# Preparing the later layers' weights beside the expert-choice routing in a five-stage audio tower

## The chip, the cores and the metric

The kernel runs on one core of one Trainium2 chip. The metric is the device time of one execution in microseconds; the time given is the median of three runs. All arithmetic is float32. Where a matmul needs full precision, an operand is rounded to a shorter format ("hi", type fp32r) and the remainder is kept beside it ("lo"); three matmuls then stand for one.

## The reference

The input x is (16, 750, 128). Five steps follow one another on h of (16, 748, 128), each but the first as h = h + f(layernorm(h)):

```python
h = tok(x, kernel)                       # convolution of width 3, then c = f*c + (1-f)*z, h = o*c
h = h + cross_attention(ln(h))           # 8 heads of 16, batch b attends to batch (b + 8) % 16
h = h + expert_choice(ln(h))             # 8 experts of 256; each takes its best 187 tokens of 748
h = h + slice_attention(ln(h))           # 8 heads of 64, 32 slices
h = h + mixture(ln(h))                   # 2 shared experts of 512, and the best 2 of 8 routed ones
```

Slice attention uses W_in, b_in, Wq, Wk, Wv, W_out and b_out. Because softmax is the only non-linear step, products of these weights are formed once (`wqk`, `fold`, and three biases). The mixture has `sw1, sw2` (shared), `rw1, rw2` (routed) and a gate. Layernorm has no learned parameters: it needs a mean and a reciprocal deviation for every token.

## The kernel before

`audio_tower` (line 2552 on) runs the stages strictly one after the other: `quasi_recurrent`, `cross_attention`, `expert_choice`, `slice_attention`, `mixture`. Each stage is made of blocks. In a block the five engines and SyncE's DMA queue have programs of their own, tied by semaphores; a block ends when all of them are done, and after a group of blocks another one clears its semaphores. So nothing of a later block overlaps an earlier one. h stays in SBUF as 96 tiles of 128 tokens (16 batches of 6 tiles); `g.stats` holds six numbers for every tile.

**Weights and statistics.** `weights_and_statistics` (line 102 on) loads weight pieces into a ring of four (line 142), turns them on TensorE where needed (line 154), rounds them to hi on ScalarE (line 170) and subtracts for lo on VectorE (line 186). A load waits until the piece four before it has its lo. With `taken` False, VectorE runs the 96 `bn_stats` (line 189) between its pieces. Lines 193 to 203 then make mean and deviation: seven small VectorE operations and a square root on ScalarE. Expert choice calls it with `taken` False, the other stages with True, because the work that made their h also took its statistics.

**Cross attention** works in 32 units (a batch and half of the heads), each of six steps. TensorE interleaves `probe` matmuls for the next unit's row maxima (line 750), score matmuls (line 770) and the sums with v (line 786). VectorE reduces every probe (line 840) out of a ring of three PSUM banks. TensorE may fill a bank only once VectorE has released the probe three places before it. After a unit's 48 probes VectorE makes `neg_max` (line 845), TensorE turns it, VectorE copies it to `max_rows` (line 850), and a DMA places it in the next unit's q stack (line 705); the next unit waits for that (`row_loaded`). GpSimd adds a unit's output to h (line 680).

**Expert choice**: weights and statistics, `router_logits`, `route`, then `gated_ffn`. `route` (line 1031 on) is one chain on VectorE: a softmax, and 24 rounds of `max` (line 1106) and `match_replace` (line 1111). ScalarE has one exponential in it, TensorE one group of transposes, GpSimd nothing, and SyncE stores the gates at its end (line 1118).

**Slice attention** begins with `slice_weights` (line 1481 on): weights and statistics, `load_small` with four loads, and a block with 8 matmuls for `wvo`, 40 for the products, and their evictions. **The mixture** begins with `expert_records` (line 1961 on): 16 weight pieces of 256 KB are turned, split into hi and lo and stored to the DRAM tensor `records` in stores of 512 KB. SyncE issues the load of piece j, then waits for the lo of piece j-2 and issues its store. Then come weights and statistics for the shared experts and the gate, one small load, a one-instruction block, `router_logits`, `dispatch` and `experts`.

Of the kernel before, what the change touches and what calls it, by code (L numbers as in the profile page):

```python
# [5 lines left out]
F32 = mybir.dt.float32  # L6
# [5 lines left out]
P = 128  # L12
# [568 lines left out]
def cross_attention(nc, g, w):  # L581

    with ExitStack() as ctx:
# [78 lines left out]
        with nc.Block() as block:  # L662
# [168 lines left out]
            def _(dve):  # L831
                def take(u, item, at, bank):
# [198 lines left out]
def route(nc, g, logits, gates, k_tokens, k_experts, tag):  # L1031
# [4 lines left out]
    with ExitStack() as ctx:  # L1036
# [21 lines left out]
        with nc.Block() as block:  # L1058
# [375 lines left out]
def expert_choice(nc, g, w):  # L1434
# [4 lines left out]
    with ExitStack() as ctx:  # L1439
# [10 lines left out]
        with ExitStack() as inner:  # L1450
# [10 lines left out]
            ], "c", False)  # L1461
            router_logits(nc, g, wg_hi, wg_lo, None, logits, "c")
            route(nc, g, logits, gates, K_TOKENS, None, "c")
# [17 lines left out]
def slice_weights(nc, g, w, wqk_hi, wqk_lo, fold, bias_q, bias_k, bias_out):  # L1481

    with ExitStack() as ctx:
        def sb(name, shape, dt=F32):
            return ctx.enter_context(nc.sbuf_tensor(name, shape, dt))

        def psum(name, shape):  # L1490
            return ctx.enter_context(nc.psum_tensor(name, shape, F32))

        sem = semaphores(nc, ctx)

        win_t = sb("win_t", [S_DIM, S_HEADS, P])
        wv_t = sb("wv_t", [S_DIM, 1, S_DIM])
        b_col = sb("b_col", [S_DIM, 1, S_HEADS])
        wqk = sb("wqk_raw", [S_DIM, 2, SLICES])
        w_out = sb("w_out_raw", [S_DIM, S_HEADS, P])
        b_out = sb("b_out_rows", [P, P])  # L1500
        b_wide = sb("b_wide", [S_DIM, S_HEADS, P])
        wvo = sb("wvo", [S_DIM, S_HEADS, P])
        weights_and_statistics(nc, g, [
            (win_t[:, :, :], None, w["L1_attn_W_in"].rearrange("d (h k) -> d h k", k=S_DIM), True),
            (wv_t[:, :, :], None, w["L1_attn_Wv"].rearrange("k (o c) -> k o c", o=1), True),
            (b_col[:, :, :], None, w["L1_attn_b_in"].rearrange("(h o k) -> h o k", o=1, k=S_DIM), True)], "d", True)
        load_small(nc, [
            (wqk[:, 0, :], w["L1_attn_Wq"], None), (wqk[:, 1, :], w["L1_attn_Wk"], None),
            (w_out[:, :, :], w["L1_attn_W_out"].rearrange("(h k) o -> k h o", k=S_DIM), None),
            (b_out[:, :], w["L1_attn_b_out"].unsqueeze(0).broadcast_to([P, P]), None)], "d")  # L1510
        p_vo = psum("p_vo", [S_DIM, 2, 4, P])
        p_qk = psum("p_qk", [P, S_HEADS, 2, SLICES])
        p_fold = psum("p_fold", [P, 2, 4, P])
        p_bq = psum("p_bq", [P, S_HEADS, SLICES])
        p_bo = psum("p_bo", [P, 2, P])
        p_bk = psum("p_bk", [P, 2])
        widened, vo_done, vo_kept, rest_done, rounded = (
            sem(s) for s in ("b_widened", "vo_done", "vo_kept", "rest_done", "wqk_rounded"))
        with nc.Block() as block:
            @block.tensor  # L1520
            def _(pe):
                for h in range(S_HEADS):
                    last = pe.matmul(p_vo[:, h // 4, h % 4, :], wv_t[:, 0, :], w_out[:, h, :], start=True, stop=True)
                last.then_inc(vo_done, 1)
                pe.wait_ge(widened, 1)
                pe.wait_ge(vo_kept, 1)
                for h in range(S_HEADS):
                    at = slice((h % 4) * SLICES, (h % 4 + 1) * SLICES)
                    pe.matmul(p_qk[:, h, :, :], win_t[:, h, :], wqk[:, :, :], start=True, stop=True)
                    pe.matmul(p_fold[:, h // 4, h % 4, :], win_t[:, h, :], wvo[:, h, :], start=True, stop=True)  # L1530
                    pe.matmul(p_bq[:, h, :], b_wide[:, h, :], wqk[:, 0, :], start=True, stop=True)
                    pe.matmul(p_bo[at, h // 4, :], b_wide[:, h, 0:SLICES], wvo[:, h, :], start=True, stop=True)
                    last = pe.matmul(p_bk[at, h // 4:h // 4 + 1], wqk[:, 1, :], b_col[:, 0, h:h + 1],
                                     start=True, stop=True)
                last.then_inc(rest_done, 1)

            @block.vector
            def _(dve):
                dve.tensor_copy(b_wide[:, :, :], b_col[:, 0, :].unsqueeze(2).broadcast_to([S_DIM, S_HEADS, P])
                                ).then_inc(widened, 1)  # L1540
                dve.wait_ge(vo_done, 1)
                dve.tensor_copy(wvo[:, :, :], p_vo[:, :, :, :].rearrange("p a b o -> p (a b) o")).then_inc(vo_kept, 1)
                dve.wait_ge(rest_done, 1)
                for j in range(2):
                    dve.scalar_tensor_tensor(out=bias_out[:, j, :], in0=b_out[:, :], scalar=1.0 / S_HEADS,
                                             in1=p_bo[:, j, :], op0=ALU.mult, op1=ALU.add)
                dve.tensor_copy(bias_k[:, :], p_bk[:, :])
                dve.tensor_copy(fold[:, :, :], p_fold[:, :, :, :].rearrange("p a b o -> p (a b) o"))
                dve.wait_ge(rounded, 3)
                for j in range(2):  # L1550
                    dve.tensor_tensor(wqk_lo[:, j, :].rearrange("p (h s) -> p h s", s=SLICES), p_qk[:, :, j, :],
                                      wqk_hi[:, j, :].bitcast(F32).rearrange("p (h s) -> p h s", s=SLICES), ALU.subtract)
                dve.tensor_tensor(bias_q[:, 1, :].rearrange("p (h s) -> p h s", s=SLICES), p_bq[:, :, :],
                                  bias_q[:, 0, :].bitcast(F32).rearrange("p (h s) -> p h s", s=SLICES), ALU.subtract)
# [1036 lines left out]
```

## Time and profile before

| | |
|---|---|
| three runs | 3235.11, 3237.22, 3238.65 us (median 3237.22) |
| the profiled execution | 3239.33 us; its span 3237.6 us |
| mean granted TensorE clock | 0.932 of full speed |
| busy, share of the span | TensorE 87%, VectorE 74%, ScalarE 58%, GpSimd 31% |

A row of the timeline begins with its start and length in us, then the engine (PE TensorE, PEld its weight loads, DVE VectorE, ACT ScalarE, POOL GpSimd, SPq SyncE's DMA queue), the line, the operation, what it writes and reads, and in brackets how long the engine was idle before it and what ended that. "x3" means that a row merges three instructions. A row of windows gives busy time and, in brackets, counts, for each engine, then the granted TensorE clock (1.00 is 2.4 GHz, 0.50 is 1.2 GHz), the DMA engines' share and GB/s.

### The profile page before, as it was taken

How to read it: one execution, taken by the hardware profiler on the slowest of the kernel's cores; microseconds unless marked ns; L12 is line 12 of the kernel's file. 1: busy time of each engine (PE TensorE's matmuls, PEld its weight loads, DVE VectorE, ACT ScalarE, POOL GpSimd, SP SyncE). 2: the span in 40 equal slices, each digit the busy share in tenths (PEclk: the TensorE clock that was granted, in tenths of full speed). 3: DMA queues.
4: the chain of work that ended last, by engine and by line, in shares of the span. 5: the costliest groups of instructions: out<-in, count | busy, mean ns of one | idle time of the engine just before them, and what ended most of it. 6: DMA issues, size and time to landing. Idle time of an engine off the chain costs nothing. (4 is left out here: it accounts for less than half of the span.)

```text
span 3237.6 us, 56270 instructions
## 1 busy us (share of the span) xinstructions
PE 2806.1 (87%) x16922; PEld 2239.5 (69%) x16922; DVE 2397.2 (74%) x4399; ACT 1872.4 (58%) x3098; POOL 1005.0 (31%) x873
## 2 busy tenths in 40 slices
PE   8975999999999999419999999588855899799994
PEld 8975665665666665319999999488844688688883
DVE  4544888888888886778999999377738666578775
ACT  3343466666666666308888888144422677577773
POOL 0033000000000000204555555233302577466664
PEclk9988899999999999759999999699967899899997
DMA  1138444355344341002322222220040211277767
GB/s 51 33 141 275 60 67 61 49 64 62 51 60 65 52 56 23 27 15 77 91 84 86 85 86 90 88 99 0 0 169 2 89 48 48 91 239 245 241 192 228
DMA packets 149262, 290.48 MB, mean 90 GB/s; under 512 B 23006, under 2 KB 77981, under 8 KB 142220
## 3 DMA queue, kind: packets, MB, share of 16 engines
q1 hardware_dynamic: 135564, 264.13, 33.4%
q0 software_dynamic: 13568, 24.75, 2.3%
q8 instruction: 65, 1.06, 0.1%
q14 instruction: 65, 0.53, 0.1%
HBM read 203.15 MB, written 87.11 MB: 90 GB/s over the span
## 5 line engine op out<-in xcount | busy, mean ns | idle before, releaser
L840 DVE TENSOR_REDUCE part_max<-to_dve 128x1 f32<-128x374 f32 (+1 forms) x1536 | 744.0, 540 | 163.3 <-PE to_dve L750 148.6
L902 ACT ACTIVATE probs<-score 128x748 f32<-128x748 f32 x768 | 579.7, 794 | 403.9 <-PE score L770 402.5
L750 PE MATMUL to_dve<-k_stack,q_stack 127*128 127x374 f32 (+1 forms) x1536 | 509.7, 377 | 30.9 <-DMA k_stack<-k_parts 30.8
L750 PEld LDWEIGHTS to_dve<-k_stack,q_stack 127*128 127x128 f32 (+1 forms) x1536 | 272.7, 190 | 299.6 <-DVE part_max L840 252.4
L2460 DVE TENSOR_TENSOR m_hid_lo<-m_hid,m_hid_hi 128x512 fp32r<-128x512 f32 x408 | 289.8, 711 | 161.3 <-ACT m_hid_hi L2433 161.3
L770 PE MATMUL score<-q_stack,k_stack 128*128 128x374 f32 x1536 | 395.1, 339 | 0.0
L1357 DVE TENSOR_TENSOR f_hid_lo_c<-f_hid_c,f_hid_hi_c 128x748 fp32r<-128x748 f32 x256 | 350.0, 1376 | 42.6 <-ACT f_hid_hi_c L1340 39.6
L680 POOL TENSOR_TENSOR h<-h,o_rows 128x256 f32 (+2 forms) x96 | 49.4, 531 | 944.9 <-DVE o_rows L863 944.9
L1253 POOL TENSOR_TENSOR f_acc_c<-f_acc_c,f_gate_c 128x748 f32<-128x748 f32 x112 | 253.1, 2259 | 259.6 <-DVE f_gate_c L1373 259.3
L786 PE MATMUL o_sum<-probs,v_sb 128*17 128x374 f32 (+1 forms) x3072 | 315.9, 483 | 16.4 <-ACT o_cols L893 14.0
L1335 ACT ACTIVATE f_hid_c<-f_up_c,c_b 128x374 f32<-128x374 f32 x512 | 268.5, 571 | 76.3 <-DVE f_hid_lo_c L1357 52.0
L770 PEld LDWEIGHTS score<-q_stack,k_stack 128*128 128x128 f32 x1536 | 274.3, 191 | 9.1 <-ACT probs L902 7.8
L2356 POOL DMA_INDIRECT e_sums<-m_gated,m_row_in x216 | 213.3, 987 | 163.8 <-DVE m_gated L2478 110.4
L2433 ACT CAST m_hid_hi<-m_hid 128x512 fp32r<-128x512 f32 x408 | 248.3, 609 | 0.0
L2350 POOL DMA_INDIRECT e_slots<-e_rows,e_places x192 | 195.5, 1018 | 103.2 <-issue 57.1
L1340 ACT CAST f_hid_hi_c<-f_hid_c 128x748 fp32r<-128x748 f32 x256 | 209.5, 819 | 9.9
L2440 ACT ACTIVATE m_hid<-m_up,m_weights 128x512 f32<-128x512 f32 x216 | 148.8, 689 | 91.1 <-PE m_up L2389 91.1
L2440 ACT ACTIVATE m_hid<-m_up,e_b 128x512 f32<-128x512 f32 x192 | 132.2, 688 | 96.4 <-PE m_up L2389 96.4
L1274 PE MATMUL f_up_c<-f_hi_c,c_w_hi 128*128 128x374 f32 x512 | 181.0, 353 | 6.5 <-ACT f_hid_c L1335 5.3
L2389 PE MATMUL m_up<-m_hi,m_weights 128*128 128x512 f32 x432 | 175.0, 405 | 0.0
L2399 PE MATMUL m_down<-m_hid_hi,m_weights 128*128 128x512 f32 x432 | 170.7, 395 | 1.4 <-DVE m_hid_lo L2460 1.4
L1274 PE MATMUL f_up_c<-f_hi_c,c_w_lo 128*128 128x374 f32 x512 | 171.4, 335 | 0.0
(412 smaller groups left out, 6170.9 us busy)
## 6 DMA issues: line engine op xcount, KB each, us to landing
m_weights<-e_records SPq DMA_DIRECT2D x54, 1028.0 KB, 6.8
f_gate_c<-c_gates SPq DMA_DIRECT2D x128, 374.0 KB, 3.4
q_stack<-q_parts SPq DMA_DIRECT2D x128, 187.0 KB, 5.4
k_stack<-k_parts SPq DMA_DIRECT2D x128, 187.0 KB, 9.4
e_slots<-blank SPq DMA_DIRECT2D x54, 260.0 KB, 3.6
m_row_in<-e_slots SPq DMA_DIRECT2D x54, 260.0 KB, 3.0
m_weights<-e_sums SPq DMA_DIRECT2D x16, 640.0 KB
e_records<-rec_parts SPq DMA_DIRECT2D x16, 512.0 KB, 3.9
```

The source lines that it names most:

```text
L750: last = pe.matmul(ring[bank][0:ROWS[c], 0:HALF], q_stack[its_slot][0:MAX_ROW, head, c * P:c * P + ROWS[c]], k_stack[its_slot][0:MAX_ROW, ...
L770: last = pe.matmul(score[e % 2][:, m, 0:HALF], k_stack[slot][:, head, c * P:(c + 1) * P], q_stack[slot][:, head, HALVES[half]], start=True ...
L786: last = pe.matmul(o_sum[head * LANE:head * LANE + VCOLS, 0:HALF], v_sb[slot][0:ROWS[c], c, head, :], probs[0:ROWS[c], s % 2, head, m, :], ...
L840: dve.tensor_reduce(part_max[0:ROWS[c], head, c, half:half + 1], ring[bank][0:ROWS[c], 0:HALF], AX.X, ALU.max).then_inc(used, 1)
L902: act.activation(probs[:, s % 2, head, :, :], score[e % 2][:, :, 0:HALF], ACT.Exp).then_inc(prob_done, 1)
L1253: pool.tensor_tensor(acc[:, slot, :], acc[:, slot, :], place, ALU.add).then_inc(summed, 1)
L1274: last = pe.matmul(up[h][:, 0:HALF], a[:, k, :], m[:, slot, cols], start=(i == 0), stop=(i == 2))
L1335: act.activation(hid[:, k % 2, cols], up[h][:, 0:HALF], ACT.Gelu, bias=b1[:, 0, k:k + 1]).then_inc(gelu_done, 1)
L1357: dve.tensor_tensor(hid_lo[:, k % RING, :], hid[:, k % 2, :], hid_hi[:, k % RING, :].bitcast(F32), ALU.subtract).then_inc(lo_done, 1)
L2433: act.copy(hid_hi[:, f % RING, :], hid[:, f % RING, :]).then_inc(hi_done, 1)
L2440: act.activation(hid[:, f % RING, :], up[f % UPS][:, :], ACT.Gelu, bias=up_bias(m, f - starts[m])).then_inc(gelu_done, 1)
L2460: dve.tensor_tensor(hid_lo[:, f % RING, :], hid[:, f % RING, :], hid_hi[:, f % RING, :].bitcast(F32), ALU.subtract).then_inc(lo_done, 1)
```

## The change

Four things are changed.

1. **Statistics of cross attention.** VectorE takes three `bn_stats` at the end of step 4 (of 0 to 5) in every unit from the third on, over tiles that two units before it finished, after a wait on GpSimd's additions; the last six follow the last unit. Expert choice calls `weights_and_statistics` with `taken` True.
2. **One list of later weights.** `later_weights` prepares everything that `slice_weights`, `expert_records` and the mixture's own call did. It returns a program for each engine, and `route` runs them in its block: on TensorE after the group of transposes, on ScalarE after the exponential, on GpSimd at once, on SyncE ahead of the wait for the gates. VectorE has no part of it.
3. **Other engines for the split.** ScalarE now copies every piece out of PSUM twice (hi, and the whole), and GpSimd subtracts. 13 small loads come first, then 20 pieces of 256 KB (4 shared, 16 routed) in a ring of four, and 16 stores. The product matmuls stand between pieces 3 and 4. PSUM has a ring of four banks for all of it.
4. **The old places.** `slice_weights`, `expert_records`, both `load_small` calls and the one-instruction block are gone. `slice_attention` and `mixture` call `weights_and_statistics` with an empty list, which leaves the operations of lines 193 to 203.

```diff
@@ cross_attention, vector engine
+                def take_tiles(first, n):
+                    for j in range(n):
+                        at = bass.ds(first + j, 1)
+                        dve.bn_stats(g.stats[:, at, :]..., g.h[:, at, :]...)
                     for s, items in enumerate(plan(u)):
                         for k, item in enumerate(items):
                             take(u, item, *number(u, s, k))
+                        if s == STEPS - 2 and at_least(u, 2):
+                            dve.wait_ge(added, u * 2)
+                            take_tiles(u * SPAN - 2 * SPAN, SPAN)        # SPAN = 3
...
+                dve.wait_ge(added, 2 * UNITS)
+                take_tiles((UNITS - 2) * SPAN, 2 * SPAN)
@@ route
             def _(sp):
+                later.sync(sp)
                 sp.wait_ge(whole, 1)
                 sp.dma_start(gates, gate_cols[:, :]).then_inc(kept, 16)
+                later.end(sp)
                 sp.wait_ge(kept, 16)
...
                 act.activation(flat, flat, ACT.Exp).then_inc(exped, 1)
+                later.scalar(act)
...
                 turn_tiles(pe, g, turn, src).then_inc(turned, 1)
+                later.tensor(pe)
+            @block.gpsimd
+            def _(pool):
+                later.gpsimd(pool)
@@ later_weights (new)
+    def sync(sp):
+        def store(n):
+            if kind == "shared":
+                return
+            sp.wait_ge(lo_done, n + 1)
+            sp.dma_start(records[x, ...], parts[:, n % RING, ...]).then_inc(stored[n % RING], 16)
+        for dst, src in small:                                            # 13 of them
+            sp.dma_start(dst, src).then_inc(small_in, 16)
+        for n, (kind, x, side) in enumerate(pieces):                      # 4 shared, 16 routed
+            if n >= RING:
+                sp.wait_ge(turned, job_of(n - RING) + 1)
+            sp.dma_start(raw[:, n % RING, :, :], view).then_inc(raw_in[n % RING], 16)
+            if n >= LATE:                                                 # LATE = 2
+                store(n - LATE)
+        for n in range(len(pieces) - LATE, len(pieces)):
+            store(n)
+        sp.wait_ge(evacuated, SMALL_JOB + 1)
+        sp.dma_start(records[:, :, 4 * HID_E:REC]..., records_bias[:, :, :]).then_inc(bias_stored, 16)
+    def end(sp):
+        sp.wait_ge(bias_stored, 16)
+        for j in range(RING):
+            sp.wait_ge(stored[j], 16 * (len(pieces) - OWN) // RING)
+    def tensor(pe):
+        pe.wait_ge(small_in, 16 * len(small))
+        ...  # 7 small transposes, 8 of W_in, pieces 0 and 1, 8 matmuls for wvo, pieces 2 and 3,
+        ...  # 40 product matmuls, pieces 4 to 19 (4 transposes each)
+    def scalar(act):
+        def round_piece(n):
+            act.wait_ge(turned, j + 1)
+            act.copy(piece_at(n)[0], heads4(j))
+            act.copy(whole[:, n % RING, :, :], heads4(j)).then_inc(evacuated, 1)
+    def gpsimd(pool):
+        def low_piece(n):
+            pool.wait_ge(evacuated, job_of(n) + 1)
+            pool.tensor_tensor(lo, whole[:, n % RING, :, :], hi.bitcast(F32), ALU.subtract).then_inc(lo_done, 1)
@@ slice_attention, mixture
-        slice_weights(nc, g, w, wqk_hi, wqk_lo, fold, bias_q, bias_k, bias_out)
+        weights_and_statistics(nc, g, [], "d", True)
-        expert_records(nc, g, w, records)
...
-            weights_and_statistics(nc, g, [ ...gate, ups, downs, sb2, sb1... ], "e", True)
-            load_small(nc, [...gate_b...], "e")
+            weights_and_statistics(nc, g, [], "e", True)
```

## Rows read from the trace of the kernel before

**Rows 1.** windows of core 0: one row for each of five stretches

```profile
318.00:1307.20 989.20, 964.78 (x6368) 587.28 (x6368) 795.96 (x1792) 595.56 (x832) 49.39 (x96) 0.98 0.43 56
1309.00:1338.60 29.60, 0.56 (x2) 0.35 (x2) 26.20 (x119) 7.57 (x15) 0.00 (x0) 0.50 0.25 72
...
1389.30:1452.10 62.80, 1.51 (x6) 1.14 (x6) 54.33 (x83) 2.12 (x2) 0.00 (x0) 0.50 0.02 6
...
2054.20:2075.60 21.40, 19.95 (x96) 18.27 (x96) 1.90 (x2) 0.00 (x0) 0.00 (x0) 0.50 0.00 1
2373.00:2439.20 66.20, 22.18 (x85) 15.53 (x85) 16.88 (x35) 13.53 (x23) 0.00 (x0) 0.51 0.61 207
```

**Rows 2.** timeline inside cross attention, from one unit to the next

```profile
884.25 1.00 DVE L840 TENSOR_REDUCE part_max<-to_dve 128x1 f32<-128x374 f32 x2
...
885.17 0.27 DVE L850 CAST max_rows<-to_dve 24x128 fp32r<-24x128 f32 x1
...
885.30 0.61 PE L750 MATMUL to_dve<-k_stack,q_stack 127*128 127x374 f32 x2
885.47 0.77 SPq L705 DMA_DIRECT2D q_stack<-max_rows  x1
...
887.91 0.37 PEld L770 LDWEIGHTS score<-q_stack,k_stack 128*128 128x128 f32 x2
```

**Rows 3.** groups of instructions, VectorE, 1308 to 1339 us: busy, mean | idle

```profile
L189 DVE BATCH_NORM_STATS2 stats<-h 128x6 f32<-128x128 f32 x96 | 19.9, 276 | 0.0
```

**Rows 4.** timeline and DMA issues (KB each, us to landing), expert choice's weights

```profile
1309.50 14.50 SPq L142 DMA_DIRECT2D raw_c<-in_L_ffn_W_dram  x12
...
1338.65 0.34 POOL L952 MEMSET c_wg_hi<- 128x120 f32 x2 [31.55 <-POOLq L54]
...
raw_c<-in_L_ffn_W_dram SPq DMA_DIRECT2D x4, 256.0 KB, 2.7
```

**Rows 5.** timeline, first and last of the routing block, and the next stage

```profile
1389.72 0.95 DVE L1069 TENSOR_REDUCE peak_c<-c_logits 128x96 f32<-128x768 f32 x1 [1.52 <-PEq L54]
...
1448.67 0.37 SPq L1118 DMA_DIRECT2D c_gates<-gate_cols_c  x1
...
1452.15 1.47 POOL L90 TENSOR_TENSOR f_rows_c<-h,mean 128x768 f32<-128x768 f32 x1 [73.55 <-POOLq L54]
```

**Rows 6.** timeline, from the block after the feed-forward to slice attention

```profile
2039.36 0.06 DVE L177 MEMSET eps_d<- 128x1 f32 x1 [2.12 <-PEq L54]
...
2044.40 0.31 DVE L193 TENSOR_TENSOR diff_d<-stats 128x96 f32<-128x96 f32 x1
...
2046.33 0.75 DVE L203 RECIPROCAL rstd<-std_d 128x96 f32<-128x96 f32 x1 [0.44 <-ACT std_d L172]
...
2079.09 0.20 POOL L1647 MEMSET first_row<- 128x128 f32 x1 [45.72 <-POOLq L54]
```

**Rows 7.** timeline, from the block after slice attention to the mixture's router

```profile
2375.56 0.11 DVE L2036 MEMSET rec_bias<- 128x64 f32 x1 [2.69 <-PEq L54]
...
2379.37 2.82 PE L2023 MATMUL rec_turn<-ident,rec_raw 128*128 128x128 f32 x12 [1.64 <-DMA rec_raw<-in_L_ffn_rw_dram]
...
2418.59 0.43 SPq L2007 DMA_DIRECT2D e_records<-rec_bias  x1
...
2439.27 0.33 POOL L952 MEMSET e_wg_hi<- 128x120 f32 x2 [75.40 <-POOLq L2542]
```

**Rows 8.** waits of SyncE's DMA queue, 2374 to 2424 us: total, times, longest

```profile
SPq L1990 <- DVE rec_parts L2043: 26.9, 14, 4.2
```

**Rows 9.** single lines: duration ns min/median/max, first and last start us

```profile
L770 PE MATMUL score<-q_stack,k_stack x1536: 327/334/515, 348.1 to 1300.2; 128*128 128x374 f32 x192
...
L962 POOL TENSOR_TENSOR r_rows_c<-r_rows_c,rstd x16: 612/613/614, 1340.9 to 1378.0; 128x256 f32<-128x256 f32 x16
...
L92 POOL TENSOR_TENSOR y_rows<-y_rows,rstd x16: 1468/1471/1473, 202.3 to 271.7; 128x768 f32<-128x768 f32 x16
...
L1357 DVE TENSOR_TENSOR f_hid_lo_c<-f_hid_c,f_hid_hi_c x256: 919/1148/2562, 1463.0 to 2027.0; 128x748 fp32r<-128x748 f32 x128
```

More of the change, by code:

```diff
@@ L1028, in _, with route @@
                                           ALU.add)
-def route(nc, g, logits, gates, k_tokens, k_experts, tag):
+def route(nc, g, logits, gates, k_tokens, k_experts, tag, later):
     N = B * TILES
@@ L1431, in _, with expert_choice @@
                 sp.wait_ge(done, 16 * len(loads))
-def expert_choice(nc, g, w):
+def expert_choice(nc, g, w, records, d, e):
     HID = 256
@@ L1460, in expert_choice @@
                 (b1[:, :, :], None, w["L0_ffn_b1"].rearrange("e (j o f) -> (e j) o f", o=1, f=P), True),
-            ], "c", False)
+            ], "c", True)
             router_logits(nc, g, wg_hi, wg_lo, None, logits, "c")
-            route(nc, g, logits, gates, K_TOKENS, None, "c")
+            with ExitStack() as beside:
+                route(nc, g, logits, gates, K_TOKENS, None, "c", later_weights(nc, beside, g, w, records, d, e))
         gated_ffn(nc, g, w1_hi, w1_lo, b1, w2_hi, w2_lo, b2, None, BLOCKS, 0, gates, None, "c")
@@ L1478 @@
 HS = S_HEADS * SLICES
[L1481 to L1554, printed above, removed]
-            @block.scalar
-            def _(act):
-                act.wait_ge(rest_done, 1)
-                for j in range(2):
-                    act.copy(wqk_hi[:, j, :].rearrange("p (h s) -> p h s", s=SLICES), p_qk[:, :, j, :]
-                             ).then_inc(rounded, 1)
-                act.copy(bias_q[:, 0, :].rearrange("p (h s) -> p h s", s=SLICES), p_bq[:, :, :]).then_inc(rounded, 1)
@@ L1565, in slice_attention, with slice_storage, sb, mixture_storage @@
-def slice_attention(nc, g, w, slots):
+def slice_storage(nc, ctx):
+    d = Shared()
+    def sb(name, shape, dt=F32):
+        return ctx.enter_context(nc.sbuf_tensor(name, shape, dt))
+    d.wqk_hi, d.wqk_lo = sb("wqk_hi", [P, 2, HS], F32R), sb("wqk_lo", [P, 2, HS], F32R)
+    d.fold = sb("fold", [P, S_HEADS, P])
+    d.bias_q = sb("bias_q", [P, 2, HS], F32R)
+    d.bias_k = sb("bias_k", [P, 2])
+    d.bias_out = sb("bias_out", [P, 2, P])
+    return d
+def mixture_storage(nc, ctx):
+    e = Shared()
+    def sb(name, shape, dt=F32):
+        return ctx.enter_context(nc.sbuf_tensor(name, shape, dt))
+    n = SHARED * UNIT
+    e.w1_hi, e.w1_lo = sb("e_w1_hi", [P, n, P], F32R), sb("e_w1_lo", [P, n, P], F32R)
+    e.w2_hi, e.w2_lo = sb("e_w2_hi", [P, n, P], F32R), sb("e_w2_lo", [P, n, P], F32R)
+    e.b1 = sb("e_b1", [P, 1, n])
+    e.b2 = sb("e_sb2", [P, 1])
+    e.gate_bias = sb("e_gate_b", [P, E_N])
+    e.wg_hi, e.wg_lo = sb("e_wg_hi", [P, 1, WIDE], F32R), sb("e_wg_lo", [P, 1, WIDE], F32R)
+    return e
@@ L2504, in _, with mixture @@
                     add_pair(b)
-def mixture(nc, g, w, slots, out):
+def mixture(nc, g, e, records, slots, out):
     N = B * TILES
-    BLOCKS = SHARED * UNIT
     with ExitStack() as ctx:
@@ L2526, in mixture @@
         with ExitStack() as inner:
[L2527 to L2529 removed]
             logits = inner.enter_context(nc.sbuf_tensor("e_logits", [P, TILES, B, E_N], F32))
[L2531 to L2546 removed]
+            weights_and_statistics(nc, g, [], "e", True)
+            router_logits(nc, g, e.wg_hi, e.wg_lo, e.gate_bias, logits, "e", rows)
             dispatch(nc, g, logits, rows, places, second, table)
[L2548 to L2549 removed]
+        experts(nc, g, records, slots, sums, rows, places, second, table, e.w1_hi, e.w1_lo, e.w2_hi, e.w2_lo, e.b1,
+                e.b2[:, 0:1], out)
 def audio_tower(nc, w, out):
@@ L2561, in audio_tower @@
         cross_attention(nc, g, w)
-        expert_choice(nc, g, w)
         slots = nc.dram_tensor("e_slots", (ROUTED * BLOCK, RECORD), F32, kind="Internal").ap()
-        slice_attention(nc, g, w, slots)
-        mixture(nc, g, w, slots, out)
+        records = nc.dram_tensor("e_records", (E_N, P, REC), F32, kind="Internal").ap()
+        e = mixture_storage(nc, ctx)
+        with ExitStack() as sliced:
+            d = slice_storage(nc, sliced)
+            expert_choice(nc, g, w, records, d, e)
+            slice_attention(nc, g, d, slots)
+        mixture(nc, g, e, records, slots, out)
 _INS = ['x', 'L0_tok_kernel', 'L0_attn_q_w', 'L0_attn_kv_w', 'L0_ffn_Wg', 'L0_ffn_W1', 'L0_ffn_b1', 'L0_ffn_W2',
```

300 lines of the change are left out of this document (193 added, 107 removed).

## The prediction

> **What bounds the kernel now.** The blocks follow one another, so a stretch of time is worth what the wait that ends last in it allows. The first view is the windows by stage [rows 1]. In cross attention TensorE is busy 965 of 989 us and VectorE 796: no VectorE work added there is free by itself. Four stretches look different. Expert choice's weights (29.6 us) have VectorE busy 26.2, TensorE nearly idle. The routing block (62.8 us) is one VectorE chain, 54.3 us busy, while the other engines and the DMA do nothing. The weights ahead of slice attention (the 41.7 us after the feed-forward) and ahead of the mixture (66.2 us, DMA share 0.61) are stages that no token needs: only their statistics depend on h. The second view is the timeline at the edges of these stretches [rows 4 to 7]. It gives what each costs from start to start, block boundaries included. The third is the timeline inside cross attention [rows 2], and the fourth SyncE's waits in the record stage [rows 8], which tell what sets the pace of the pieces.
>
> **Slice attention's weights, removed.** GpSimd's first operation of slice attention stands at 2079.09, the block after the feed-forward opens at 2039.36 [rows 6]. With an empty list the block has only the statistics. These took from 2044.40 to 2047.08 [rows 6], 2.7 us, and one boundary follows. For its price I take 1.06 us, what lies between the end of expert choice's statistics, 1337.59, and 1338.65, the next stage's first operation [rows 4]. The new start is 2039.36 + 0.1 + 2.7 + 1.06 = 2043.2, so the change gives 35.9 us. After it the low clock is no new cost: the granted clock is 0.50 in the old stretch even with TensorE busy 20 of 21.4 us [rows 1], so slice attention started cold already.
>
> **The mixture's preparation, removed.** By the same sum: block open at 2375.56, router's first operation at 2439.27 [rows 7], new start 2375.56 + 3.84 = 2379.4. It gives 59.9 us. Both sums have an uncertainty of 1 to 2 us, the boundaries.
>
> **Expert choice without `bn_stats`.** 96 of them are 19.9 us of VectorE, 0.207 each [rows 3], in a stage of 29.6. Not all of it comes back, because the loads are next late. A load waits for the lo four pieces before it. SyncE's first twelve issues took 14.5 us [rows 4]. In the chain of piece 0, 4, 8 and 12 a link of 128 KB is about 3.1 us (landing, 0.4 of ScalarE, 0.4 of VectorE), and the last, of 256 KB, about 4.8 (2.7 us landing [rows 4], behind three like it). Piece 0 has its lo some 2 us after the first issue, at 1311.1. So: 1311.1 + 3.1 + 3.1 + 4.8 = 1322.1, then 0.6 for the two bias copies and 2.7 of statistics, 1325.4 instead of 1337.6. I take a gain of 12.2 us; ends 10 (every landing 0.5 later) and 19.9 (VectorE still the bound).
>
> **The same `bn_stats` in cross attention.** The last six follow the last addition to h, outside any cover: 6 x 0.207 = 1.3 us. The other 90 come three to a unit, 0.62 us, after `neg_max`. What is queued behind them on VectorE are the first two probes of step 5 and `max_rows`, and TensorE waits for these through the ring. VectorE took the two probes at 884.25, TensorE issued the next two at 885.30 [rows 2]. It may do so when each of the first two is released, at about 884.75 and 885.25, so the slack is 0.2 us at the second. With 0.62 to 0.75 more (0.75 if the address arithmetic does not run ahead) TensorE loses 0.4 to 0.55. The maxima's row is the other path: issued at 885.47, it is needed at 887.91 [rows 2]. A DMA of that size should land near 887.5; it moves by 0.62 and TensorE by 0.45, so it stays just hidden. TensorE has next to no idle time in this stage, so a stall is not won back. I take 0.5 us in each of 29 units, 14.5 us. The ends are 0 (three banks cover it) and 0.95 a unit (all of it, plus a late row), 28 us.
>
> **The new work in routing.** Here the question is whether it fits beside the chain of VectorE, which runs from 1389.72 to 1448.6 [rows 5]. SyncE begins with 13 small issues. One costs between 0.37 [rows 5] and 0.77 [rows 2]; I take 0.5, 6.6 us. TensorE waits for all 13: with 2.3 us of landing (2.7 for 256 KB [rows 4]) it starts at 1398.6. Ahead of the first routed piece stand 31 transposes at 2.82/12 = 0.235 us [rows 7], 7.3 us, and the 48 matmuls of the products, which took 20 of the 21.4 us [rows 1]. First routed piece: 1425.9. The 16 routed pieces took from 2379.37 to 2418.59 before, 39.2 us or 2.45 a piece [rows 7]. They have the same bytes now, three loads are again ahead of them, and SyncE has the same order. SyncE waited for lo there, 26.9 us in 14 times [rows 8], so the path from load to lo sets the pace, at least in part. It grows by ScalarE's second copy (0.5) and by GpSimd in place of VectorE. GpSimd takes 0.61 us for 256 elements and 1.47 for 768 [rows 9], hence 1.04 for 512, against 0.69. That is 0.85 in a loop that carries three pieces, with handing over some 1.0: up to 0.33 a piece. If the DMA alone sets the pace it is 0. I take 0.2: 3.2 us, and 1.1 once for the longer last piece. The last store is out at about 1469.5. The gates' store stands behind it on SyncE: issue at 1470. From that issue to GpSimd's next stage it was 3.5 us (1448.67 to 1452.15 [rows 5]); 1.0 more for stores still in flight and 1.0 for one more block that clears semaphores give 1475.4 instead of 1452.15. The work does not fit: it costs 23.3 us, of which the 59 us beside VectorE are the cover used. Ends: 12 (DMA pace, issues of 0.4) and 33 (0.33 a piece, 10 us of small issues, a GpSimd that also waits). VectorE itself has 20 us to spare here.
>
> GpSimd and VectorE run side by side for the first time in this block. With GpSimd's additions running in the feed-forward, VectorE's two-input subtraction goes from 919 ns to a median of 1148 and up to 2562 [rows 9]. If the rounds of `max` and `match_replace` were stretched likewise, VectorE's chain would grow by at most GpSimd's own busy time, some 25 us, to about 1474: just the end that SyncE has anyway. So it costs nothing more either way. The Trainium skill (SBUF — State Buffer, the sections on the shared port pair) says that only VectorE operations with two SBUF inputs or in a two-port mode contend with GpSimd, and that a loser blocks for a whole instruction. By it the rounds, one input each, are not stretched; without it the sum is the same. No row of this trace has a `max` beside GpSimd.
>
> **Sum.** -35.9 - 59.9 - 12.2 + 1.3 + 14.5 + 23.3 = -68.9 us. From the profiled execution's own 3239.3 us (its span 3237.6 and 1.7 around it) that is 3170.4. The median of the three runs is 2.1 us below the profiled one, hence 3168.
>
> **The rivals.**
> - *The ring covers the statistics.* Then cross attention pays only 1.3 us: 3168 - 14.5 = 3154. For it: VectorE is idle for a fifth of the stage, 796 busy of 989 us [rows 1]. Against: the slack at the place where the three stand is 0.2 us [rows 2]. Chance 0.18.
> - *They cost all and the row comes late.* 0.8 to 0.95 a unit, 3177 to 3181. For it: the row's landing isn't shown, and 2.4 us is close. Chance 0.14.
> - *Routing hides more.* If the small issues are short, the products are faster in their new grouping, and the DMA sets the pace, the excess falls to 8 to 12 us: 3153 to 3157. Hiding all of it would need the routed pieces at 1.4 us each, with 768 KB moved for each, and these rows show 2.45 [rows 7]. Chance 0.14.
> - *Routing stretches more*, to 30 us or above, because GpSimd's subtractions are slower than 1.04: 3175 to 3182. Chance 0.10.
> - *The other side: cross attention loses its clock.* The stage stands on a granted clock of 0.98 [rows 1]. If the new stalls made the grant drop for part of it, a score matmul goes from 334 to 515 ns [rows 9], and TensorE-bound time grows by at least half of the stretch so spent. To eat the gain of 69 us some 140 of the 989 us must fall to the low level, 4 to 5 us in every unit. That gives 3237 and more; less than that stays a gain. Against: the stage keeps 0.98 although TensorE waits in every unit already, and the added stall is 0.5 us in 30. Chance 0.02.
> - *The change doesn't do what it says*: the later weights end up behind the routing instead of beside it. In part this is my forecast; if all of it stood behind (86 us), the time would be about 3232. The programs start without waiting for VectorE's rounds, so I give it 0.01.
>
> **How the numbers follow.** The forecast itself, 3168 with its own spread of 6 either way, has 0.41. The cases below it reach to 3147, those above to 3186, and the range from 3147 to 3186 leaves out about 0.15. Faster by over 0.2%, about what a measurement of this kernel can tell from no change, is all but two rivals: 0.97; within it 0.01; slower 0.02.
>
> **What would show it.** Cross attention's stretch should be some 16 us longer, with TensorE's probes of step 5 late behind `max_rows`. Expert choice's weights should last about 16 to 17 us. In routing, VectorE should be done at about 59 us from its first operation and then idle for some 20 while SyncE still stores records; a next stage that starts within 5 us of VectorE's last operation would prove the excess wrong. From block opening to slice attention, and to the mixture's router, it should be some 4 us each. The forecast is wrong if a unit of cross attention grows by less than 0.2 or more than 0.9 us, or if the pieces come faster than 2.3 or slower than 3.0 us.

## The result, and the profile after

The changed kernel takes **3228.0 us** (median of 14 runs, 3222.1 to 3236.3) against 3236.1 before (14 runs, 3233.6 to 3238.7): a ratio of 0.9975, with a 95% interval of 0.9967 to 0.9982. That is 8 us faster, where 68 were forecast. Its profiled execution took 3223.5 us, with a span of 3221.4. One run of an experiment below, of after_no_stats, took 9296.7 us; it is left out of its figures as slow, and nothing here tells why.

Stage by stage, from the timelines of both kernels (us; before by [rows 1, 4 to 7], after by the rows below):

| stage | before | after | change | forecast |
|---|---|---|---|---|
| cross attention, up to expert choice's weights | to 1309.2 | to 1390.2 | +81.0 | +15.8 |
| expert choice's weights, to the router's first operation | 29.5 | 17.9 | -11.6 | -12.2 |
| routing block, to the feed-forward's first operation | 62.4 | 80.1 | +17.6 | +23.3 |
| feed-forward to slice attention's first operation | 39.7 | 3.8 | -36.0 | -35.9 |
| slice attention to the mixture's router | 63.7 | 3.8 | -59.9 | -59.9 |
| all others (mixture -6.0, feed-forward -0.9, routers and slice attention -0.4) | | | -7.3 | 0 |

The sum is -16.2, the difference of the two spans. It is more than the 8 us between the medians, because the profiled execution of before lies 3 us above its median and that of after 4.6 below. The mixture's 6.0 are in part scatter: over all profiles here it took 794.0 to 798.3 us in the five with its old code (mean 796.1) and 791.4 to 794.2 in the nine with the new (mean 793.3); what the other 3 us are was not looked for. So the changed stages came near the forecast, routing 6 us better, and the gain went into cross attention. After's timeline where these stages begin and end (start, us of the row, engine, line, operation):

```profile
1390.20 0.06 DVE L177 MEMSET eps_c<- 128x1 f32 x1 [2.02 <-PEq L54]
...
1406.25 0.75 DVE L203 RECIPROCAL rstd<-std_c 128x96 f32<-128x96 f32 x1 [0.44 <-ACT std_c L172]
...
1408.06 0.34 POOL L965 MEMSET c_wg_hi<- 128x120 f32 x2 [21.18 <-POOLq L54]
...
1458.96 0.95 DVE L1082 TENSOR_REDUCE peak_c<-c_logits 128x96 f32<-128x768 f32 x1 [1.52 <-PEq L54]
...
1539.02 1.47 POOL L90 TENSOR_TENSOR f_rows_c<-h,mean 128x768 f32<-128x768 f32 x1 [6.89 <-POOLq L54]
...
2125.34 0.06 DVE L177 MEMSET eps_d<- 128x1 f32 x1 [1.66 <-PEq L54]
...
2129.10 0.21 POOL L1856 MEMSET first_row<- 128x128 f32 x1 [8.94 <-POOLq L54]
...
2425.32 0.06 DVE L177 MEMSET eps_e<- 128x1 f32 x1 [2.22 <-PEq L54]
...
2429.09 0.33 POOL L965 MEMSET e_wg_hi<- 128x120 f32 x2 [14.99 <-POOLq L54]
```

**Where cross attention grew.** Taking the starts of `max_rows`, one in every unit, a unit lasts 30.10 us before. After, it is 31.05 (+0.95), and every third unit 36.9 to 38.6: eight units with 6.6 us more on average. 28 x 0.95 + 8 x 6.6 = 79, and behind the last unit, where the last six `bn_stats` are, it is 1.1 us longer. After's timeline at the first long unit:

```profile
500.35 1.00 DVE L848 TENSOR_REDUCE part_max<-to_dve 128x1 f32<-128x374 f32 x2 [0.37 <-PE to_dve L750]
507.14 2.36 DVE L848 TENSOR_REDUCE part_max<-to_dve 128x1 f32<-128x374 f32 x5 [5.79 <-issue]
...
501.84 0.82 PE L786 MATMUL o_sum<-probs,v_sb 128*17 128x374 f32 x8
507.74 1.13 PE L750 MATMUL to_dve<-k_stack,q_stack 127*108 127x374 f32 x2 [5.08 <-DVE part_max L848]
```

VectorE stands still for 5.79 us, and the releaser is "issue": it waited for nothing that the profile knows. TensorE waits for it. The record of VectorE's sequencer has `COMPARE_BRANCH`, the jump back of its loop, at 500.605, and its next record at 507.001. Waits of VectorE from 400 to 1260 us (total, times, longest), and the DMA queue of instructions in the same stretch (packets, MB), after:

```profile
DVE part_max L848 <- PE to_dve L750: 114.7, 272, 1.4
DVE part_max L848 <- issue: 43.1, 8, 5.8
DVE stats L837 <- issue: 9.5, 25, 0.5
```

```profile
q14 instruction: 44, 0.36, 0.2%
```

and the same queue and stretch before:

```profile
q14 instruction: 6, 0.05, 0.0%
```

Eight pauses at eight jumps back, and 38 packets of 8 KB more: five for each turn of VectorE's loop, the first of them inside the pause. The packets carry no engine's name, but they keep time with this loop alone: VectorE was fetching its own loop again in every turn. Each pause also cost TensorE its clock, which is granted at half (1.2 GHz) from 506.2 to 513.0 us and again in full from there:

```profile
501.00:508.00 7.00, 1.92 (x14) 0.96 (x13) 1.21 (x3) 1.55 (x2) 0.00 (x0) 0.87 1.07 132
508.00:515.00 7.00, 6.61 (x32) 4.10 (x31) 4.59 (x10) 3.29 (x5) 0.00 (x0) 0.64 0.63 94
515.00:522.00 7.00, 7.00 (x55) 4.35 (x48) 5.52 (x12) 4.24 (x7) 0.00 (x0) 1.00 0.00 0
```

(windows of after: busy us of PE, PEld, DVE, ACT and POOL, then the granted clock, the DMA share and GB/s). After four of the eight pauses the half clock stood for 6.8 us, after the other four for 3.4. So a long unit is longer by 0.8 to 1.9 us more than its pause: the first has 7.6 for a pause of 5.8.

### The profile page after: what moved, and what is told of

It is laid out like the page before. It is cut to its first block and busy times, and to the rows that moved or that the text cites. A ratio compares the mean times of both kernels' runs of the same rounds, so it can differ in the third digit from the quotient of the medians.

```text
span 3221.4 us, 56390 instructions
## 1 busy us (share of the span) xinstructions
PE 2818.8 (88%) x16922; PEld 2242.8 (70%) x16922; DVE 2377.8 (74%) x4359; ACT 1889.4 (59%) x3136; POOL 1033.8 (32%) x901
## 5 line engine op out<-in xcount | busy, mean ns | idle before, releaser
L750 PE MATMUL to_dve<-k_stack,q_stack 127*128 127x374 f32 (+1 forms) x1536 | 525.0, 385 | 85.2 <-DVE part_max L848 53.8
L750 PEld LDWEIGHTS to_dve<-k_stack,q_stack 127*128 127x128 f32 (+1 forms) x1536 | 279.5, 192 | 367.2 <-DVE part_max L848 320.3
L1378 DVE TENSOR_TENSOR f_hid_lo_c<-f_hid_c,f_hid_hi_c 128x748 fp32r<-128x748 f32 x256 | 348.6, 1371 | 43.5 <-ACT f_hid_hi_c L1361 41.5
L1307 PE MATMUL f_down_c<-f_hid_hi_c,c_w_hi 128*128 128x374 f32 x512 | 171.3, 335 | 0.0
L1295 PE MATMUL f_up_c<-f_lo_c,c_w_hi 128*128 128x374 f32 x512 | 171.2, 334 | 0.0
```

The lines of the kernel that those rows point to most:

```text
L750: last = pe.matmul(ring[bank][0:ROWS[c], 0:HALF], q_stack[its_slot][0:MAX_ROW, head, c * P:c * P + ROWS[c]], k_stack[its_slot][0:MAX_ROW, ...
L1295: last = pe.matmul(up[h][:, 0:HALF], a[:, k, :], m[:, slot, cols], start=(i == 0), stop=(i == 2))
L1378: dve.tensor_tensor(hid_lo[:, k % RING, :], hid[:, k % 2, :], hid_hi[:, k % RING, :].bitcast(F32), ALU.subtract).then_inc(lo_done, 1)
```

## Experiments on the long units

Three theories. **A**: instructions come in blocks, only a few blocks are kept, and a jump back is free only where the whole loop lies in them; so its place counts. **B**: the length of the loop alone counts (353 VectorE instructions before, 383 after, the sequencer's included). **C**: the statistics, their semaphore or GpSimd's additions stall VectorE. The edit of all `ahead` runs is the same, N instructions in a stretch of 10 us in which VectorE waits for the first probe:

```
                 dve.wait_ge(zeroed, 2)
+                for k in range(N):
+                    dve.memset(pad[:, k:k + 1], 0.0)
                 for k, item in enumerate(opening):
```

**before_ahead64**: the kernel before, N = 64.

> The kernel before, with no statistics in cross attention, and 64 short VectorE instructions ahead of its loop of 353. Theory A: at the new place the loop overruns the window, and every third unit of cross attention becomes 6 to 8 us longer, without one bn_stats: 3236 + 54 = 3290. Theories B and C: nothing changes, 3236. If the stall shows here, the statistics have no part in it.

3289.9 us, ratio 1.0156 (1.0139 to 1.0173). Ordinary units stay at 30.10, eight are 36.3 to 37.6, 6.9 more on average. The stall is there without one `bn_stats` in the stage: C falls.

**after_ahead128** and **after_ahead64**:

> The changed kernel with 128 short VectorE instructions (memsets of one column) put ahead of VectorE's loop in cross attention, in a stretch where VectorE waits 10 us anyway; the loop itself is untouched. In the changed kernel a unit lasts 31.05 us instead of 30.10, and the eight units with a backward jump of VectorE's loop last 36.9 to 38.6 us, 6.7 more. Theory A (the jump target must still lie in a window of fetched instructions, and the window is laid out in fixed blocks of the program, so the place of the loop decides): 127 instructions further on the loop of 383 straddles fewer blocks, the 6.7 us are gone, eight times, and the kernel gains some 54 us: about 3174. Theory B (the length of the loop body alone decides, with its limit between 353 and 383 instructions): nothing changes, 3228. Theory C (the stall comes from the statistics themselves, their semaphore or GpSimd's additions): nothing changes, 3228.

> The same with 64 short instructions ahead of the loop. Theory A: by the sizes that lie between (353 instructions fit at their place, 383 do not at the same place), a loop moved by only 63 instructions lies worse, not better, if a block is 256 instructions: the eight long units stay, 3228. With blocks of 128 or less it could fit again. Theories B and C: no change, 3228. Told apart from the run with 128, this shows that not the added instructions but the place counts.

3224.4 (ratio 0.9957, 0.9941 to 0.9974) and 3216.5 us (0.9931, 0.9915 to 0.9948): the long units stay in both, so the blocks are not those of the first expectation. But with 64 ahead the ordinary unit fell to 30.68, which no theory had foreseen. The records of VectorE show why. Once in every 128 of its instructions, at the same place of the program modulo 128, it takes 0.35 to 0.37 us more to go on. In the changed kernel that is ahead of instructions 100, 228 and 356 of the loop (counted from 0), with 128 ahead of the loop at 101, 229 and 357, in both cases among the instructions of the three `bn_stats`, where TensorE waits. With 64 ahead they fall among the probes and are covered. I read these as the borders of blocks of 128 instructions, each one packet of 8 KB. (Written out without a loop, as in before_straight below, VectorE has 63 instructions a unit, and a packet comes every 60.7 us, two units: one for 127 instructions.) Counted from them (N memsets move the loop by N - 1):

```
kernel             loop begins, ends   blocks of 128   long units
before                28     381             3              0
before_ahead8         35     388             4              8
before_ahead64        91     444             4              8
before_ahead128       27     380             3              0
after                 28     411             4              8
after_ahead64         91     474             4              8
after_ahead128        27     410             4              8
after_ahead101         0     383             3              0
after_ahead108         7     390             4              8
```

**before_ahead128**:

> The kernel before with 128 short VectorE instructions ahead of its loop of 353. With 64 of them every third unit had become 7.3 us longer and the kernel 52 us slower; with none it is not so. Theory A1 (VectorE's instructions are kept in blocks of 128, 8 KB, the size of each packet on the instruction queue in the trace, and a jump back is free only where the loop lies in three blocks): 127 further on is one short of a whole block, so the loop lies as it did without them: no long units, 3237. Theory A2 (blocks of 256): at 128 it lies as badly as at 64, or worse: 3290. Theory D (the added instructions do it, not the place): the stall stays, 3290.

3236.4 us, ratio 1.0003 (0.9993 to 1.0013), no long unit. It isn't the added instructions, it is the place.

**after_ahead101**, **after_ahead108** and **before_ahead8**: their lines of the table were worked out before they ran.

> The changed kernel with 101 short VectorE instructions ahead of its loop in cross attention (64 and 128 did not remove the long units). In the traces so far VectorE pauses 0.37 us once in every 128 of its instructions, always at the same place of the program modulo 128; that gives the borders of the blocks. Counted from these, the loop begins 28 instructions into a block and ends at 381 in the kernel before (three blocks are 384) and at 411 in the changed one. Theory A1 (a jump back is free where the loop lies in three blocks of 128): 101 instructions ahead put its first instruction at 0 and its end at 383: no long units, 8 x 6.7 = 53 us gained. And the border no longer falls between the three bn_stats, so that a unit costs 30.68 instead of 31.05 us, as with 64 ahead: another 10 us. 3228 - 63 = 3165. Rival A3 (a body over some 360 to 380 never fits, wherever it lies): 3217, as with 64 ahead.

> The same with 108, seven instructions more than in the run with 101. Theory A1: the loop now ends at 390 of 384, and needs a fourth block: the eight long units are back, 3217 to 3221. Rival A3: the same as with 101, whatever that is. Seven memsets of 0.06 us cannot cost 50 us in any other way.

> The kernel before with eight short VectorE instructions ahead of its loop. Theory A1: its loop ends at 381 of 384 today; seven further on it ends at 388, so every third unit becomes 7.3 us longer: 3236 + 52 = 3288, from eight memsets. If the kernel stays at 3236, blocks of 128 and a limit of three are not the rule, though they fit the six runs before.

3165.8 us (ratio 0.9781, 0.9766 to 0.9796), 3218.5 (0.9946, 0.9931 to 0.9962) and 3297.7 (1.0189, 1.0174 to 1.0205). Seven memsets more or less are worth 53 us, and eight memsets make the kernel before 63 us slower (3234.9 in the same session). B falls with these: 383 instructions fit at one place, 353 don't at another. VectorE's waits from 400 to 1260 us and the instruction queue in before_ahead8:

```profile
DVE part_max L841 <- issue: 53.1, 8, 7.0
```

```profile
q14 instruction: 45, 0.37, 0.2%
```

and the queue in after_ahead101, whose waits have no row with "issue" on VectorE:

```profile
q14 instruction: 7, 0.06, 0.0%
```

One miss is a size: before_ahead8 pauses 6.1 to 7.0 us at a time where the others pause 4.4 to 6.1, and has 6.8 us of half clock each time, so its long units are 8.1 us longer, not 7.3. What sets the length of a pause was not tried. Another thing stays open: in after_ahead108 most of the ordinary units last 31.1 to 31.6 us again and not 30.68, with borders ahead of instructions 121 and 249, soon behind `max_rows`. The Trainium skill (Runtime: NRT & Kernel Launch, Instruction fetch mechanics) has the mechanism: a taken branch to a page that isn't in the window waits for a fetch. Its sizes, 16 KiB blocks of 256 instructions and a window of two, don't fit. Such blocks would have their borders at every second border of the table, in one of two ways. One way would let after_ahead108 and after_ahead128 go free, the other after, after_ahead64, before_ahead8 and before_ahead64. All six stalled, so here the measured rule holds: three blocks of 128.

## Experiments on the price of the statistics, and on routing

**after_straight**: VectorE's program of the stage without a loop.

```
-                steps3(dve, UNITS, 2, 3, step)
+                for u in range(UNITS):
+                    step(u, u % 3)
```

> The changed kernel with VectorE's program of cross attention written out for all 32 units, without a loop: no jump, and no address or count is worked out at run time. Theory A and B: no stall at the third units, since instructions are fetched in order: gain 54 us. C: the stalls stay. Besides, the three bn_stats then follow each other without the gaps of 0.1 to 0.3 us in which their addresses were worked out: their price in a unit falls from 0.95 to about 0.6 to 0.7 us, another 8 to 10 us. Together about 3165.

3155.5 us, ratio 0.9746 (0.9730 to 0.9762), some 10 below what was expected. No long units, and a unit is 30.27, where 30.7 to 30.8 had been expected. **before_straight**, the same edit in the kernel before:

> The kernel before with VectorE's program of cross attention written out for all 32 units. It tells whether the gain of the changed kernel written out (3155.5) is in part that of writing out. If the loop costs the kernel before nothing, a unit stays at 30.10 us and the time at 3236 (3232 to 3240), and all of the 81 us belongs to the change. If working out counts and addresses was on TensorE's path, a unit falls by 0.1 or more and the time by 3 us or more.

3234.6 us, ratio 0.9996 (0.9987 to 1.0006): writing out is worth nothing by itself, though a unit falls to 30.01. So the statistics cost 0.26 us a unit there, and 0.95 in the changed kernel. The timelines tell the difference, after's loop first:

```profile
963.40 0.20 DVE L853 TENSOR_REDUCE neg_max<-part_max 128x24 f32<-128x48 f32 x1
...
963.74 0.29 DVE L837 BATCH_NORM_STATS2 stats<-h  x1
...
964.34 0.53 DVE L837 BATCH_NORM_STATS2 stats<-h  x2 [0.31 <-issue]
964.78 0.98 DVE L848 TENSOR_REDUCE part_max<-to_dve 128x1 f32<-128x374 f32 x2
```

then after_straight:

```profile
917.58 0.20 DVE L853 TENSOR_REDUCE neg_max<-part_max 128x24 f32<-128x48 f32 x1
917.70 0.67 DVE L837 BATCH_NORM_STATS2 stats<-h 128x6 f32<-128x128 f32 x3
918.28 0.99 DVE L848 TENSOR_REDUCE part_max<-to_dve 128x1 f32<-128x374 f32 x2
```

From `neg_max` to the next probe it is 1.38 us in the loop and 0.70 written out, against 0.24 before the change, whose rows are these:

```profile
883.43 0.55 DVE L840 TENSOR_REDUCE part_max<-to_dve 108x1 f32<-108x374 f32 x1 [0.40 <-PE to_dve L750]
884.01 0.20 DVE L845 TENSOR_REDUCE neg_max<-part_max 128x24 f32<-128x48 f32 x1
884.25 1.00 DVE L840 TENSOR_REDUCE part_max<-to_dve 128x1 f32<-128x374 f32 x2
```

Less the slack of 0.2, the additions of 1.14 and 0.46 give 0.94 and 0.26. With 64 ahead the same distance is 1.02, which gives 0.58. The 0.95 is thus 0.26 for three `bn_stats`, 0.32 for working out their addresses in registers, and 0.37 for the border of a block that happens to lie between them.

**after_no_stats**: all of the change but its statistics, which expert choice's weights take as before.

> The changed kernel with the statistics of h taken in expert choice's weights, as before, and none in cross attention: all of the change but its statistics. From the two traces: slice attention's weights 36.0 less, the mixture's preparation 59.9 less, the routing block 17.6 more, the remaining stages alike. Cross attention should be back at 30.10 us a unit without long ones, and expert choice's weights at 29.5 us. Sum 78.3: 3236 - 78 = 3158. If part of the growth of cross attention came from something else in the change, it stays in the units.

3154.2 us (median of three runs, 3152.6 to 3165.2), ratio 0.9764 (0.9742 to 0.9785). All units are at 30.10, expert choice's weights at 29.6 us, the routing block at 78.3. The moved statistics are what turned a gain of some 76 us, by that ratio, into 8: they give back 11.6 and cost 81.

**after_straight_late3**: stores beside routing one load later (`RING, LATE = 4, 3`), VectorE written out.

> The changed kernel with VectorE's cross attention written out (3155.5 us), and in the work beside routing the store of a piece issued behind three further loads instead of two. In the changed kernel the 16 routed pieces take 2.74 us each, and the routing block 80.1 us, 20 of them behind VectorE's last operation. Theory P (the pace is the way of three pieces round SyncE, DMA, TensorE, ScalarE and GpSimd, some 8.2 us): with four pieces in the loop it falls to about 2.1 us, 16 x 0.6 = 10 us less: 3146. Rival Q (the DMA or an engine sets the pace): 2.7 us a piece stay, 3155.

3149.1 us, ratio 0.9726 (0.9710 to 0.9742), which overlaps with that of after_straight. The pace fell as theory P says, from 2.60 us a piece in after_straight to 2.05 (GpSimd's subtractions, the sixth to the last), but the routing block only from 79.2 to 77.7. TensorE's wait for loads, after and late3:

```profile
PE l_bank L1647 <- DMA l_raw<-in_L_ffn_rw_dram: 24.1, 13, 4.9
```

```profile
PE l_bank L1648 <- DMA l_raw<-in_L_ffn_rw_dram: 15.9, 12, 4.5
```

What took the gain was the clock. In the profiles of after and after_straight TensorE was granted 2.4 GHz for 6.8 us at the start of the products (after's window 1469 to 1479), in that of late3 it stood at 1.2 GHz throughout (1402 to 1413). GpSimd began the first routed piece's low part 37.8 us after the block's opening, against 32.2 in after_straight:

```profile
1469.00:1479.00 10.00, 10.00 (x75) 9.22 (x75) 9.66 (x16) 8.39 (x25) 7.07 (x9) 0.84 0.42 132
```

```profile
1402.00:1413.00 11.00, 11.00 (x52) 10.34 (x50) 10.62 (x17) 5.00 (x11) 5.09 (x5) 0.50 0.23 72
```

after_ahead101, with the routing code of after, drew the same lot: 38.3 us to that subtraction, and a block of 86.4. With the grant, the version below, also with late stores, has a block of 71.7. Why the grant comes in some executions and not in others stays open.

**after_straight_spread_late3**: besides, each `bn_stats` alone at a place where VectorE waits for a probe, with `PLACES = [(4, 6), (5, 2), (5, 6)]` for step and item.

```
                             take(u, item, *number(u, s, k))
+                            if (s, k) in PLACES and 2 <= u < UNITS - 2:
+                                if (s, k) == PLACES[0]:
+                                    dve.wait_ge(added, u * 2)
+                                take_tiles(u * SPAN - (2 * SPAN - PLACES.index((s, k))), 1)
-                        if s == STEPS - 2 and at_least(u, 2):
+                        if s == STEPS - 2 and u >= UNITS - 2:
                             dve.wait_ge(added, u * 2)
                             take_tiles(u * SPAN - 2 * SPAN, SPAN)
```

> A version meant to be faster than both: the changed kernel with VectorE's cross attention written out, the three bn_stats of a unit put singly where VectorE waits some 0.4 us for TensorE's next probe anyway (ahead of the last probe of step 4, ahead of the fourth and of the eighth of step 5) instead of together behind neg_max, and the stores beside routing one load later. With the bn_stats together a unit is 30.27 us against 30.01 without them, both written out. If the waits cover them singly, a unit is back at 30.01 to 30.10: 28 x 0.2 = 5 to 7 us less than after_straight_late3 (3149): 3143. If a bn_stats is longer than the wait it stands in (0.21 and its gaps against 0.34 to 0.42), a unit stays at 30.2 to 30.3 and the time at 3149.

**3135.7 us**, ratio 0.9697 (0.9683 to 0.9710): the fastest version, 3% under the kernel before. A unit is 29.99 us, as without statistics:

```profile
880.23 1.91 DVE L849 TENSOR_REDUCE part_max<-to_dve 128x1 f32<-128x374 f32 x4 [0.22 <-PE to_dve L750]
882.06 0.28 DVE L838 BATCH_NORM_STATS2 stats<-h 128x6 f32<-128x128 f32 x1
882.56 0.55 DVE L849 TENSOR_REDUCE part_max<-to_dve 108x1 f32<-108x374 f32 x1 [0.22 <-PE to_dve L750]
883.14 0.20 DVE L854 TENSOR_REDUCE neg_max<-part_max 128x24 f32<-128x48 f32 x1
```

The probe behind the `bn_stats` still waits 0.22 us for TensorE, where before the change this wait was 0.40 (row 883.43): the instruction stands in it and costs nothing. Of the 13 us under late3 cross attention gave 8.0 (it ends at 1308.8, not 1316.8). The rest is the routing block, 71.7 us, which drew the full clock in its products again. That part is luck and no merit of the edit; without these 6 us the time would be near the 3143 that were expected.

## Why the prediction was wrong

**The step that failed** is "The same `bn_stats` in cross attention". It priced the added instructions by their run time and by who waits for them, and took the loop's code for free. The loop had three instructions to spare in its three blocks (381 of 384), the change adds 30, and 8 x 6.6 = 53 us come from that alone. No rival named it: apart from the one on the clock, all stayed within 0 to 0.95 us a unit, and "a unit grows by more than 0.9 us" was the sign of being wrong. With 53 us more, the forecast of 3168 would have been 3221. after_ahead101 and after_ahead108, seven memsets apart, show these 53 us by themselves (3165.8 and 3218.5).

**Its size without that** was taken as 0.5 us a unit; it was 0.95, the end of the bound, but not for the reason given there. The slack of 0.2 was right (1.14 and 0.46 both lose 0.2), the 0.62 to 0.75 for the triplet was 0.78 with its addresses, and the border came on top. The row of the maxima wasn't late: TensorE waited for it once in the stage, 0.6 us, after as before. (The sum has 29 units; the edit puts three `bn_stats` in 30, of which the last two show 0.2 us and less.) The rival "they cost all" thus had the right number for this part, 13 us above the forecast, by luck: its cause was another.

**The rival on the clock** was right that a stall costs TensorE its grant, but the stalls that did it were the pauses, not the half microsecond that it had in mind, and the low level stood for 41 us of the stage in all, not the 140 that it needed. What the long units took beyond their pauses, 10 us in all, is the most that it can have cost: the smaller part of a long unit.

**Slice attention's weights and the mixture's preparation**: -36.0 and -59.9, as worked out, within 0.1. The new starts are 3.8 us behind the opening of their blocks.

**Expert choice's weights**: -11.6 instead of -12.2. VectorE was busy for 8.6 of the 18 us. ScalarE waited 14.0 us for loads, and SyncE 6.1 for the lo parts, as the sum had it.

**Routing** cost 17.6, not 23.3, and the terms erred in both directions. The small issues took 6.2 us (6.6), TensorE began 9.4 us after the opening (8.9), but the first routed piece was turned at 29.3 us, not 36.2: the products took less than the 20 us of the old order, in part at the full clock. The sixteen pieces took 44.3 us to the last store, for which 43.5 were summed: a subtraction on GpSimd takes 1.27 us for 512 elements, not the 1.04 between its rows for 256 and 768. From the last store of the records (issued at 1532.54) to the next stage it was 6.5 us, for which 5.9 were summed. VectorE's chain ended 58.9 us after the opening, as before, and SyncE, behind GpSimd, set the end:

```profile
SPq L1611 <- POOL l_parts L1755: 43.9, 16, 16.3
SPq L1623 <- PE l_bank L1647: 8.3, 5, 5.0
```

**GpSimd beside VectorE**: `max` took 940 to 942 ns in after as in before, so one-input operations weren't stretched. Nor was `match_replace`, at 921 ns in both. The one two-input operation that VectorE has behind the rounds met a subtraction on GpSimd, and that took 1.96 us where its fellows take 1.27:

```profile
1516.94 0.94 DVE L1125 SCALAR_TENSOR_TENSOR gate_cols_c<-work_c,cols_c 128x748 f32<-128x748 f32 x1
...
1517.04 1.96 POOL L1755 TENSOR_TENSOR l_parts<-l_whole,l_parts 128x512 fp32r<-128x512 f32 x1 [1.42 <-ACT l_whole L1710]
```

By the rule quoted from the Trainium skill (SBUF — State Buffer, SBUF: two separate sides), the trace agrees: VectorE's operation, which began first, had 0.84 us left and wasn't stretched, and GpSimd's took 0.69 longer.

**The scatter** of the changed kernel, 14 us where the kernel before has 5, fits eight pauses that last 4.8 to 5.8 us within one execution, and a grant in the products that some executions have and others don't; neither was tried by itself.

## What to carry to other kernels

Before adding instructions to a loop on an engine, count what its body has already, the sequencer's register operations included, and look for what the code's place gives: in the trace, a pause with the releaser "issue" behind each jump back, and packets on the instruction queue in a steady loop, meant here that the loop no longer fitted. Then write the loop out, shorten it or move it; a time that changes by 63 us for eight memsets ahead of a loop is no measure of anything that stands inside it. And small work for an engine that is idle in part belongs singly into waits that the timeline shows, not in one piece in front of what another engine needs.

## What the runs showed of the hardware

- VectorE's instructions came in blocks of 128 (8 KB a packet). A loop ran without fetching where it touched three blocks, in four kernels of four (three of the table and after_no_stats, whose loop lies as before's), and fetched in every turn where it touched four, in six of six. A jump back then cost 4.4 to 7.0 us of pause, and 5.7 to 8.1 us of the stage on average.
- Passing the border of a block cost VectorE 0.35 to 0.37 us, seen only where nothing covered it: the same loop gave units of 31.05 us in after and 30.68 in after_ahead64.
- Each of TensorE's 48 stops at a jump back, 3.7 to 6.3 us long in the six kernels with long units, brought 3.4 or 6.8 us at 1.2 GHz, which began within the stop or up to 1.2 us behind it, in a stage that otherwise held 2.4 GHz.
- Three `bn_stats` with addresses worked out at run time took 0.78 us more between their neighbours (after_ahead64), with fixed ones 0.46 (after_straight).
- The stretch of products beside routing, some 10 us, drew 2.4 GHz for 6.8 us in seven of the nine profiles that have it, and not in those of late3 and after_ahead101, where the first routed piece came some 6 us later.
